# Attention weights of the first key block in a ring of six units instead of four, and a second table of rotations turned only when it can be taken up

## The chip, the cores and the metric

The kernel runs on one core of a Trainium2 chip. The metric is the device time of one execution in microseconds (us), lower is better. Its engines, as the profile names them: PE (TensorE, matrix products; PEld is its weight load), DVE (VectorE), ACT (ScalarE), POOL (GpSimd), SP (SyncE, which here only starts transfers, DMAs). SBUF is the working memory, PSUM the eight banks of 512 fp32 columns into which PE writes.

## The reference

Four batch elements of 512 rows by 512 features (`x`) go through eight blocks, each `x = layernorm(x + block(x))`: a small state-space network (width 64, four layers), a four-bit linear map, then attention 1, a gated FFN, attention 2, a routed mixture of low-rank experts, attention 3 and a wide gated FFN (1792). The three attentions have 32 query heads, 8 key/value heads and a head width of 16; all three are causal. Cut to the attention:

```python
q = rope(x @ Wq); k = rope(x @ Wk); v = x @ Wv        # 32, 8, 8 heads of 16
scores = einsum("bkgqd,bkmd->bkgqm", q, k) / sqrt(16)  # attention 1: / 16
scores = where(causal, scores, -inf)
out = einsum("bkgqm,bkmd->bkgqd", softmax(scores), v) @ Wo
```

## The kernel before, in words

**Stages.** The batch elements run one after the other through each attention, so there are 12 pairs (attention, element), numbered n = 0 to 11 (`NIT`). Each n has 8 groups, one for each key/value head with its four query heads; group g = 8n + head, 96 in all. First come the state-space layers and the four-bit map of the four elements (called quarters q in the layers), last the wide FFN. The dense products, FFNs and projections of the neighbouring n are dealt out between the groups of n as side work (`side_work`).

**One group.** The scores are computed twice. The first time (`max_scores`, units `max`, 10 for each group, 20 for each pair p of groups) DVE takes their maxima (L2144); for a unit with the diagonal ACT first writes a mask into the bank (`mask_first`, "preset", L1720). The maxima of a pair are split (`split_max`), turned by PE (`turn_shift`), copied (`take_shift`) and sent through DRAM back into extra rows of the queries. The second time (`exp_scores`, units `exp`, 10 a group, L1420) PE computes scores less their maximum, and ACT takes the exponential into `probs` (`weights_of`, L1731). Units 0 to 3 hold key block 0 (one head each, 512 queries), units 4 to 7 the key blocks 1 and 3, units 8 and 9 key block 2. POOL clears what is above the diagonal (`cut`, L1959), and PE multiplies by the values (`weigh`, L1435) in two halves: half 0 takes key block 0 (`pv` 0), half 1 the others (`pv` 1). ACT copies the result out (`out_heads`, L1739).

**The room for the weights.** `probs` holds ten units of 512 columns, unit i in place i. So unit i < 4 of group g may be written only when half 0 of group g - 1 is through PE, and unit i > 3 when half 1 is:

```python
if g:
    act.wait_ge(made["pv_full"], counted("pv_full", g - 1, int(i > 3)))
```

**The layers.** For each layer l and quarter q: statistics (DVE `hs`, L2114 to L2120), POOL `hr`, scaling (ACT `hx`, L1631), a turn (PE `th`, L1309, out to SBUF by ACT), the scan (DVE `mod`, L2127 to L2129), then PE `hm` (L1337), again statistics and a turn, and the widening (PE `f`, L1343, two a layer) and narrowing products (PE `hd`, L1348 and L1352). The final turn gives `last` (L1360), the output product. The four accumulators of the layers hold four of the eight banks, so the turns and `f` have the other four.

**The rotation tables.** The tables of cosines and sines arrive as rows (`ropet`), are turned by PE into a bank (`turn_tables`, units `tabs`, L1309) and copied by ACT into `cs` (`rotations`, L1754 to L1757). Table 1 serves attention 1, table 2 attention 2 and 3. ACT may copy table 2 only after the last rotation of n = 3, since `cs` is in use until then.

**Order of the work.** Nothing is scheduled at run time: every engine has a fixed list, and a wait holds all that stands behind it in the list. The lists are made when the program is built, by `Flow.try_out`: it deals the steps of the plan out with assumed durations (`pieces`), takes on each engine the step that could begin first, and honours the dependences in `order_of` and the room in the eight banks (`room`): a step that needs a bank takes one whose last content has been taken up (`released`). `tabs` and the layers' steps may go ahead of the plan (`AHEAD`). For a bank that is given by the planner the program waits on the step that releases it (`bank_for`).

Of the kernel before, what the change touches and what calls it, by code (L numbers as in the profile page):

```python
# [9 lines left out]
ACT = mybir.ActivationFunctionType  # L10
# [60 lines left out]
def exp_unit(i):  # L71

    if i < 4:
        return [(0, i, 0)]
    if i < 8:
        return [(1, i - 4, 0), (3, i - 4, 3 * P)]
    return [(2, 2 * (i - 8), 0), (2, 2 * (i - 8) + 1, 2 * P)]
# [271 lines left out]
def order_of(engine, name, k):  # L349
# [84 lines left out]
    if name == "probs":  # L434
        return [("exp_full", k), ("pv_full", (n - 1, int(k[1] > 3))) if n else ("y_full", ("l", 0, TJ - 1))]
# [45 lines left out]
    if name == "tabs":  # L481
        return [("load_rope", k)]
# [433 lines left out]
def program(nc, ins, out, kinds):  # L916
    assert list(kinds) == ALL
    flow = FLOW
    with ExitStack() as ctx:
        def sb(name, shape, dt):  # L920
            return ctx.enter_context(nc.sbuf_tensor(name, shape, dt))
# [48 lines left out]
        ropet = sb("ropet", [P, TJ, 2, 64], F32)  # L970
# [6 lines left out]
        a = sb("a", [P, D], F32)  # L977
        t1 = sb("t1", [P, S], F32)
        t2 = sb("t2", [P, S], F32)
        r = sb("r", [P, CH, S], F32)  # L980
# [10 lines left out]
        big1 = sb("big1", [P, 14336], F32)  # L991
# [3 lines left out]
        probs = big1[:, 7680:12800]  # L995
        qp = big1[:, 12800:14336].bitcast(BF16).rearrange("p (k s t) -> p k s t", k=2, s=3)
# [12 lines left out]
        wgu = big1[:].rearrange("p (g c k n) -> p g c k n", g=M3 // 2, c=DC, k=2)  # L1009
# [69 lines left out]
        def probs_of(key):  # L1079

            lo, hi, at = ((0, 2048, 0), (2048, 4096, 0), (4096, 5120, 0), (2048, 4096, 3 * P))[key]
            return probs[:, lo:hi].rearrange("p (h t) -> p h t", h=GQ)[:, :, at:at + S - key * P]
# [4 lines left out]
        def _(sp):  # L1087
# [19 lines left out]
            def load_rope(A):  # L1107
                if A > 1:
                    sp.wait_ge(made["tabs_full"], counted("tabs_full", 1))
                sp.dma_start(ropet[:], ins[f"attn{A}_rope"]).then_inc(rope_in, 16)  # L1110
# [187 lines left out]
        def _(pe):  # L1298
# [113 lines left out]
            def exp_scores(g, i):  # L1412
                p = g // 2
                if i == 0 and g % 2 == 0:
                    pe.wait_ge(shift_in[p % 3], 16 * (p // 3 + 1))
                    if g == 0:
                        pe.wait_ge(ready, 1)
                bank = bank_for("exp", g, i)
                for key, h, at in exp_unit(i):
                    mm = pe.matmul(bank[:, at:at + S - key * P], kt[0:SROWS, p % 3, g % 2, key * P:(key + 1) * P],  # L1420
                                   qt[0:SROWS, g % 6, h, key * P:S], start=(at == 0), stop=True, skip_group_check=True)
                mm.then_inc(made["exp_full"], 1)

            def weigh(g, half_):
# [8 lines left out]
                for key in (1, 3, 2) if half_ else (0,):  # L1433
                    for h in range(GQ):
                        mm = pe.matmul(bank_of("pv", g)[32 * h:32 * h + 32, key * P:S], vs[:, n % 2, key, g % 8, :],  # L1435
                                       probs_of(key)[:, h], start=(key == 0), stop=(key == 2), skip_group_check=True)
# [179 lines left out]
        def _(act):  # L1616
# [107 lines left out]
            def weights_of(g, i):  # L1724
                n = g // 8
                if g:
                    act.wait_ge(made["pv_full"], counted("pv_full", g - 1, int(i > 3)))
                elif i == 0:
                    act.wait_ge(made["y_full"], counted("y_full", "l", 0, TJ - 1))
                act.wait_ge(made["exp_full"], counted("exp_full", g, i))  # L1730
                act.activation(probs[:, i * S:(i + 1) * S], bank_of("exp", g, i), ACT.Exp,  # L1731
# [83 lines left out]
            def squares(n):  # L1815
                act.wait_ge(made["xn"], counted("xn", "d", n))
                act.wait_ge(made["lo"], counted("lo", NIT - 1, CHUNKS[-1]))
                for j in range(TJ):
# [3 lines left out]
                    act.activation(a[:, 0:D], x_rows(n, j), ACT.Square, accum_out=ssq[:, k:k + 1]).then_inc(made["sq"], 1)  # L1822
# [80 lines left out]
        def _(pool):  # L1903
# [51 lines left out]
            def cut(g, key):  # L1955

                pool.wait_ge(made["probs"], counted("probs", g, KEY_ENDS[key]))
                block_ = probs_of(key)[:, :, 0:P]
# [614 lines left out]
```

## Time and profile before

| | before |
| --- | --- |
| median of 3 runs | 2340.5 us (2339.69 to 2342.32) |
| the profiled execution: its own time | 2339.58 us |
| its span in the trace | 2337.9 us |
| PE busy (products) | 2211.4 us, 95% of the span |
| DVE, ACT, POOL busy | 1423.1, 1237.7, 509.3 us |
| mean granted clock of TensorE | 0.972 |

The span is the time from the first to the last instruction; the 1.7 us between it and the execution's own time are outside the program. A busy PE in these views has modelled ends: products are pipelined, and each is shown somewhat longer than it keeps the next from starting. The granted clock is given as a share of full speed (2.4 GHz); its lower level is half of it.

### The profile page before, as it was taken

The page shows a single profiled execution, that of the slowest core. Times are in us where ns is not written, and L with a number is a line of the kernel's source. Part 1 is how long each engine was busy: PE and PEld are TensorE (multiplying, and loading weights), DVE is VectorE, ACT ScalarE, POOL GpSimd, SP SyncE. Part 2 cuts the span into 40 slices and gives each one's busy share as a digit, 9 for nine tenths or more (in the row PEclk, how much of TensorE's full clock was granted, in tenths as well). Part 3 has the DMA queues.
Part 4 walks back from the last instruction along what each step waited for, and adds up shares of the span by engine and source line. Part 5 has one row for each costly group of instructions (what it writes and reads, how often), then busy time and mean ns, then how long its engine had stood idle before and what let it go on. Part 6 is the DMA issues. An engine that isn't in the chain of part 4 may idle for free.

```text
span 2337.9 us, 35726 instructions
## 1 busy us (share of the span) xinstructions
PE 2211.4 (95%) x12528; PEld 1175.9 (50%) x12528; DVE 1423.1 (61%) x3153; ACT 1237.7 (53%) x2313; POOL 509.3 (22%) x646
## 2 busy tenths in 40 slices
PE   6788798999999999999999999999998999999998
PEld 5565454545455454555555555554543444444443
DVE  7756778867768586687878887878832222221222
ACT  6466597756657475676767675787761101011010
POOL 4422233223313132232323231322220000000000
PEclk8779899999999999999999999999999999999999
DMA  5001233412313132332423243333222000000000
GB/s 183 1 1 38 82 100 109 154 51 82 111 40 121 36 118 66 97 105 70 128 68 110 67 127 106 119 97 102 74 83 71 5 14 0 18 0 5 14 0 18
DMA packets 135777, 163.24 MB, mean 70 GB/s; under 512 B 42272, under 2 KB 97696, under 8 KB 135328
## 3 DMA queue, kind: packets, MB, share of 16 engines
q1 hardware_dynamic: 135600, 160.97, 22.3%
q8 instruction: 101, 1.65, 0.3%
q14 instruction: 76, 0.62, 0.1%
HBM read 94.19 MB, written 53.35 MB: 63 GB/s over the span
## 4 chain that ended last, share of the span: by engine, by line
PE 81%; DVE 6%; ACT 4%; DMA 4%; issue 2%; SPq 1%; POOL 1%; POOLq 0%; ACTq 0%; DVEq 0%
PE ps L1537 16%; PE ps L1435 9%; PE ps L1465 8%; PE ps L1548 8%; PE ps L1420 7%; PE ps L1444 7%; PE ps L1490 5%; PE ps L1390 3%; PE ps L1395 3%; PE ps L1499 2%; PE ps L1522 2%; PE ps L1309 2%; PE ps L1475 2%; PE ps L1401 2%; ACT big L1731 1%
## 5 line engine op out<-in xcount | busy, mean ns | idle before, releaser
L2144 DVE TENSOR_REDUCE peaks<-ps 128x4 f32<-128x512 f32 x960 | 623.3, 681 | 213.7 <-PE ps L1390 114.6
L1731 ACT ACTIVATE big<-ps 128x512 f32<-128x512 f32 x960 | 548.2, 603 | 295.0 <-PE ps L1420 219.9
L1959 POOL TENSOR_SCALAR_AFFINE_SELECT big<-big 128x512 f32<-128x512 f32 x384 | 257.0, 682 | 869.3 <-ACT big L1731 868.0
L1537 PE MATMUL ps<-xt,big 128*128 128x512 f32 x896 | 390.1, 593 | 2.9 <-issue 2.9
L1420 PE MATMUL ps<-big 99*128 99x512 bf16 (+3 forms) x1536 | 337.9, 300 | 12.4 <-DMA big<-scr_shift 4.6
L1537 PEld LDWEIGHTS ps<-xt,big 128*128 128x128 f32 x896 | 168.8, 190 | 209.2 <-issue 208.0
L1840 ACT ACTIVATE t<-ps 128x512 f32<-128x512 f32 x56 | 33.5, 598 | 453.4 <-PE ps L1537 453.4
L1465 PE MATMUL ps<-xt,big 128*128 128x512 f32 x480 | 246.1, 607 | 1.4 <-ACT xt L1746 1.1
L1435 PE MATMUL ps<-big,vs 128*32 128x512 f32 (+3 forms) x3072 | 239.5, 439 | 6.7 <-POOL big L1959 5.6
L1720 ACT ACTIVATE ps<-cbf 128x512 f32<-128x512 bf16 x384 | 230.4, 605 | 19.2 <-DVE peaks L2144 15.4
L2200 DVE SCALAR_TENSOR_TENSOR t<-rest,t 128x512 f32<-128x512 f32 x56 | 38.7, 691 | 280.1 <-PE ps L1537 275.7
L1420 PEld LDWEIGHTS ps<-big 99*128 99x128 bf16 x1536 | 133.0, 97 | 131.3 <-issue 67.5
L1390 PEld LDWEIGHTS ps<-big 96*128 96x128 bf16 x1536 | 112.4, 98 | 156.5 <-issue 115.6
L1548 PE MATMUL ps<-wf,big 128*128 128x512 f32 x384 | 167.8, 593 | 1.6 <-DVE big L2201 1.6
L1390 PE MATMUL ps<-big 96*128 96x128 bf16 x1536 | 150.8, 220 | 4.5 <-ACT ps L1720 4.0
L1395 PE MATMUL ps<-big 96*128 96x256 bf16 x768 | 148.5, 275 | 4.2 <-DVE peaks L2144 2.3
L1435 PEld LDWEIGHTS ps<-big,vs 128*32 128x32 f32 x3072 | 80.8, 109 | 105.4 <-issue 81.9
L1490 PE MATMUL ps<-xt,wf 128*128 128x512 f32 x256 | 125.4, 607 | 0.0
L1947 POOL TENSOR_TENSOR sm<-sm,half 128x1 f32<-128x1 f32 x16 | 8.7, 543 | 527.1 <-DVE sm L2220 527.1
L1395 PEld LDWEIGHTS ps<-big 96*128 96x128 bf16 x768 | 68.2, 99 | 102.1 <-issue 90.1
L1548 PEld LDWEIGHTS ps<-wf,big 128*128 128x128 f32 x384 | 72.6, 190 | 92.5 <-issue 89.9
L1444 PE MATMUL ps<-big 128*128 128x512 f32 x192 | 98.3, 611 | 5.9 <-DVE big L2172 5.9
(232 smaller groups left out, 2917.8 us busy)
## 6 DMA issues: line engine op xcount, KB each, us to landing
big<-scr_q SPq DMA_DIRECT2D x96, 384.0 KB, 4.0
scr_q<-big SPq DMA_DIRECT2D x48, 384.0 KB, 2.9
scr_q<-big SPq DMA_DIRECT2D x48, 256.0 KB, 3.0
recb<-scr_sums SPq DMA_DIRECT2D x96, 128.0 KB
big<-scr_k SPq DMA_DIRECT2D x48, 192.0 KB, 3.3
big<-in_ffn_gu SPq DMA_DIRECT2D x14, 512.0 KB, 5.1
scr_q<-big SPq DMA_DIRECT2D x48, 128.0 KB, 2.9
ctxt<-ots SPq DMA_DIRECT2D x192, 32.0 KB, 2.0
```

The costliest lines, as they stand in the source:

```text
L1390: mm = pe.matmul(bank_of("max", p, u)[:, h * P:(h + 1) * P], of(h, at), against(at, at + 1), start=False, stop=True, skip_group_check=True)
L1395: mm = pe.matmul(bank[:, 2 * P * k:2 * P * (k + 1)], of(at, 2 + k), against(0, 2), start=(k == 0), stop=True, skip_group_check=True)
L1420: mm = pe.matmul(bank[:, at:at + S - key * P], kt[0:SROWS, p % 3, g % 2, key * P:(key + 1) * P], qt[0:SROWS, g % 6, h, key * P:S], start=( ...
L1435: mm = pe.matmul(bank_of("pv", g)[32 * h:32 * h + 32, key * P:S], vs[:, n % 2, key, g % 8, :], probs_of(key)[:, h], start=(key == 0), stop ...
L1444: mm = pe.matmul(bank_of("dense", n, j), heads[n % 2][:, c, j * P:(j + 1) * P], wd[:, c, :], start=(c == 0), stop=(c == DC - 1))
L1465: mm = pe.matmul(bank_of("proj", n, c), wp[:, k, c * P:(c + 1) * P], xt[:, k, :], start=(k == 0), stop=(k == DC - 1))
L1490: mm = pe.matmul(bank_of(kind, n, m), wf1[:, c, at + m * P:at + (m + 1) * P], xt[:, c, :], start=(c == 0), stop=(c == DC - 1))
L1537: mm = pe.matmul(bank_of(kind, n, m), wgu[:, m // 2, c, way, m % 2 * P:(m % 2 + 1) * P], xt[:, c, :], start=(c == 0), stop=(c == DC - 1))
L1548: mm = pe.matmul(bank_of("down3", n, j), ht3[:, m, j * P:(j + 1) * P], wdn[:, m, :] if m < 12 else wdn2[:, m - 12, :], start=(m == 0), sto ...
L1731: act.activation(probs[:, i * S:(i + 1) * S], bank_of("exp", g, i), ACT.Exp, scale=1.0 / 16 if attn_of(n) == 1 else 0.25).then_inc(made["p ...
L1959: pool.affine_select(block_, block_, [[0, GQ], [1, P]], ALU.is_ge, zero, base=0, channel_multiplier=-1).then_inc(made["cut"], 1)
L2144: dve.tensor_reduce(to, blocks, AX.X, ALU.max, negate=True).then_inc(made["negmax"], 1)
```

## The change

Five things are changed; the computation is the same.

1. `probs` has twelve units of room instead of ten. Key block 0 has six places: an even group writes its units 0 to 3 to places 0, 1, 2, 3, an odd group to places 4, 5, 2, 3 (`place`), with the heads dealt so that the four places that hold a group's block stand side by side (`exp_unit`, `probs_of`). Units 4 to 9 have places 6 to 11.
2. The exponential of units 0 and 1 therefore waits for half 0 of group g - 2; units 2 and 3 still for half 0 of group g - 1, units 4 to 9 for its half 1.
3. The turn of the second rotation table has a new dependence in the planner: it comes after the last rotation of n = 3, as ACT's copy of it does.
4. To make room for the two units (4 KB in each partition), `ropet` lies in `t2` and the scratch of the squares `a` is replaced by a half of `cs`.
5. The lists of all engines are made anew with the new dependences.

```diff
+def place(g, i):
+    return i + 2 if i > 3 else i if g % 2 == 0 else (4, 5, 2, 3)[i]
+
-def exp_unit(i):
+def exp_unit(g, i):
     if i < 4:
-        return [(0, i, 0)]
+        return [(0, place(g, i) - 2 * (g % 2), 0)]
...
     if name == "probs":
-        return [("exp_full", k), ("pv_full", (n - 1, int(k[1] > 3))) if n else ("y_full", ("l", 0, TJ - 1))]
+        return [("exp_full", k), ("pv_full", (n - 1 - int(k[1] < 2), int(k[1] > 3))) if n > int(k[1] < 2) else ("y_full", ("l", 0, TJ - 1))]
...
     if name == "tabs":
-        return [("load_rope", k)]
+        return [("load_rope", k)] + ([("rope", (NB - 1, CHUNKS[-1]))] if n == 2 else [])
...
-        ropet = sb("ropet", [P, TJ, 2, 64], F32)
-        a = sb("a", [P, D], F32)
+        ropet = t2[:].rearrange("p (j w k) -> p j w k", j=TJ, w=2)
...
-        big1 = sb("big1", [P, 14336], F32)
+        big1 = sb("big1", [P, 15360], F32)
...
-        def probs_of(key):
-            lo, hi, at = ((0, 2048, 0), (2048, 4096, 0), (4096, 5120, 0), (2048, 4096, 3 * P))[key]
+        def probs_of(g, key):
+            first = 1024 * (g % 2)
+            lo, hi, at = ((first, first + 2048, 0), (3072, 5120, 0), (5120, 6144, 0), (3072, 5120, 3 * P))[key]
...
             def weights_of(g, i):
                 n = g // 8
-                if g:
-                    act.wait_ge(made["pv_full"], counted("pv_full", g - 1, int(i > 3)))
-                elif i == 0:
+                back = g - 1 - int(i < 2)
+                if back >= 0:
+                    act.wait_ge(made["pv_full"], counted("pv_full", back, int(i > 3)))
+                else:
                     act.wait_ge(made["y_full"], counted("y_full", "l", 0, TJ - 1))
                 act.wait_ge(made["exp_full"], counted("exp_full", g, i))
-                act.activation(probs[:, i * S:(i + 1) * S], bank_of("exp", g, i), ACT.Exp,
+                act.activation(probs[:, place(g, i) * S:(place(g, i) + 1) * S], bank_of("exp", g, i), ACT.Exp,
...
-                    act.activation(a[:, 0:D], x_rows(n, j), ACT.Square, accum_out=ssq[:, k:k + 1]).then_inc(made["sq"], 1)
+                    act.activation(cs[:, 0, :], x_rows(n, j), ACT.Square, accum_out=ssq[:, k:k + 1]).then_inc(made["sq"], 1)
```

No instruction is added or removed on any engine; what changes is the order. The new file is seven lines longer in the engines' part, so L1309 of before is L1315 of the change, L1343 is L1349, L1352 is L1358, L1360 is L1366, L1390 is L1396, L1395 is L1401, L1720 is L1726, L1731 is L1738 and L1739 is L1746.

**The turn of table 2, on PE.** Before, among the layers (the turn of the table reads `ropet`; the turn with `wf` is a layer's, `th`):

```order
L1348 MATMUL ps<-wf,ident 128x256 [waits f_ft]
L1352 MATMUL ps<-wf,big1 128x64 x8
L1309 MATMUL ps<-ident,ropet 128x128 [waits f_ut,rope_in]
L1309 MATMUL ps<-ident,ropet 128x128 x3
L1309 MATMUL ps<-ident,wf 128x128 [waits f_rotations,f_hx]
L1309 MATMUL ps<-ident,wf 128x128 x3
```

With the change, between dense products of n = 1 and maxima of n = 2, in group 19 of 96:

```order
L1450 MATMUL ps<-big2 128x512
L1426 MATMUL ps<-big1 128x512 [waits f_cosine]
L1450 MATMUL ps<-big2 128x512 [waits f_probs,dense_in,f_ctn]
L1315 MATMUL ps<-ident,t2 128x128 [waits f_probs,rope_in]
L1315 MATMUL ps<-ident,t2 128x128 x3
L1396 MATMUL ps<-big1 128x128 [waits f_preset]
L1396 MATMUL ps<-big1 128x128 x3
```

The turn moved from the 31st step of PE's list to the 813th. ACT's copy of table 2 keeps its place in ACT's list.

**The first pair's maxima, on PE.** `big1` alone is a unit of maxima, `ident,wf` or `ident,big2` a layer's turn that waits for ACT's scaling (`f_hx`), `ident,x` the turn of element 1 for its projections, which waits for its normalization (`f_nx`), `wf,big2` 128x512 an output product `last`, `big2` L1337 a mixing step. Before:

```order
L1337 MATMUL ps<-sm,big2 128x64 [waits f_sel,f_mod]
L1337 MATMUL ps<-sm,big2 128x64 x3
L1390 MATMUL ps<-big1 128x128 [waits f_preset]
L1390 MATMUL ps<-big1 128x128 x3
L1309 MATMUL ps<-ident,wf 128x128 [waits f_y16,f_hx]
L1309 MATMUL ps<-ident,wf 128x128 x3
L1395 MATMUL ps<-big1 128x256 [waits f_hx]
L1395 MATMUL ps<-big1 128x256
L1390 MATMUL ps<-big1 128x128 [waits f_preset]
L1390 MATMUL ps<-big1 128x128 x3
L1395 MATMUL ps<-big1 128x256 [waits f_negmax]
```

With the change:

```order
L1396 MATMUL ps<-big1 128x128 [waits f_preset]
L1396 MATMUL ps<-big1 128x128 x3
L1366 MATMUL ps<-wf,big2 128x512 [waits f_ft,w_out,f_ut]
L1366 MATMUL ps<-wf,big2 128x512 [waits f_negmax,w_out,f_ut]
L1401 MATMUL ps<-big1 128x256 [waits f_negmax]
L1401 MATMUL ps<-big1 128x256
L1396 MATMUL ps<-big1 128x128 [waits f_preset]
L1396 MATMUL ps<-big1 128x128 x3
L1401 MATMUL ps<-big1 128x256 [waits f_negmax]
L1401 MATMUL ps<-big1 128x256
L1366 MATMUL ps<-wf,big2 128x512 [waits f_negmax,w_out,f_ut]
L1315 MATMUL ps<-ident,x 128x128 [waits f_negmax,f_nx]
```

A layer's turn (quarter 2's final one) stood behind unit 3 of the maxima; it now stands before the four-bit products of element 1, and output products of element 2 have its place. The next turn of the layers (quarter 3) comes after unit 6 and one turn of element 1. All along the layers the steps of quarters 1 to 3 stand further ahead: before the first output product (L1360) there are six more of them (two turns, three widening products, one narrowing product), before the first unit of maxima six (two turns, two widening products, a mixing step and a narrowing product, the scan on DVE for it too), and before the first `exp` unit a narrowing product, a turn and two units of maxima. From group 48 to group 79 PE's list is the same as before.

**Around the end of a group, on ACT.** L1731 is an exponential, L1739 the copy of a group's result, L1720 a mask. Before, at group 50:

```order
L1720 ACTIVATE ps<-cbf 128x512 [waits f_negmax]
L1720 ACTIVATE ps<-cbf 128x512 [waits f_cosine]
L1787 ACTIVATE big1<-r 128x512 [waits parts_out1,f_rope]
L1731 ACTIVATE big1<-ps 128x512 [waits f_exp_full,f_pv_full]
L1720 ACTIVATE ps<-cbf 128x512 [waits f_probs]
L1791 ACTIVATE big1<-rest 128x512 [waits f_rest]
L1739 ACTIVATE ots<-ps 128x512 [waits heads_in,sums_in,f_pv_full]
```

With the change:

```order
L1726 ACTIVATE ps<-cbf 128x512 [waits f_negmax]
L1738 ACTIVATE big1<-ps 128x512 [waits f_exp_full,f_pv_full]
L1726 ACTIVATE ps<-cbf 128x512 [waits f_cosine]
L1794 ACTIVATE big1<-r 128x512 [waits parts_out1,f_rope]
L1726 ACTIVATE ps<-cbf 128x512 [waits f_probs]
L1798 ACTIVATE big1<-rest 128x512 [waits f_rest]
L1746 ACTIVATE ots<-ps 128x512 [waits heads_in,sums_in,f_pv_full]
```

The next group's first exponential moved ahead of a mask and of the first part of a rotated chunk.

## Rows read from the trace of the kernel before

**Rows 1.** The page: PE's busy time, and the granted clock in 40 slices.

```profile
PE 2211.4 (95%) x12528; PEld 1175.9 (50%) x12528; DVE 1423.1 (61%) x3153; ACT 1237.7 (53%) x2313; POOL 509.3 (22%) x646
...
PEclk8779899999999999999999999999999999999999
```

**Rows 2.** Windows: stretch and length; busy us of each engine; granted clock; DMA share, GB/s.

```profile
40.00:200.00 160.00, 121.99 (x562) 87.00 (x562) 106.64 (x347) 93.11 (x192) 65.99 (x73) 0.77 0.01 2
200.00:300.00 100.00, 76.64 (x387) 48.55 (x385) 70.74 (x185) 59.34 (x106) 28.74 (x34) 0.86 0.23 70
300.00:480.00 180.00, 168.32 (x1312) 89.38 (x1316) 150.50 (x298) 147.08 (x271) 56.73 (x76) 1.00 0.39 124
480.00:1440.00 960.00, 949.01 (x6452) 513.13 (x6440) 717.98 (x1441) 619.07 (x1140) 257.37 (x318) 1.00 0.28 86
1440.00:1750.00 310.00, 293.76 (x2264) 154.80 (x2262) 226.39 (x443) 229.70 (x437) 82.73 (x116) 0.99 0.33 100
```

**Rows 3.** PE timeline in the middle: start us, duration us, instruction, count.

```profile
718.88 1.02 PE L1465 MATMUL ps<-xt,big 128*128 128x512 f32 x2
...
719.75 0.38 PE L1395 MATMUL ps<-big 96*128 96x256 bf16 x2
...
719.97 0.38 PE L1420 MATMUL ps<-big 99*128 99x512 bf16 x1
```

**Rows 4.** The waits of ACT from 480 to 1440 us: total us, times, longest.

```profile
ACT big L1731 <- PE ps L1435: 56.1, 35, 3.7
```

**Rows 5.** The tile `ropet`: duration ns min/median/max, first and last start us.

```profile
L1309 PE MATMUL ps<-ident,ropet x8: 421/421/421, 51.2 to 68.1; 128*128 128x128 f32 x8
```

**Rows 6.** The tile `cs`, ACT's copies of both tables, same columns.

```profile
L1754 ACT ACTIVATE cs<-ps x2: 577/578/580, 56.2 to 593.0; 64x512 f32<-64x512 f32 x2
```

**Rows 7.** The waits of PE from 40 to 200 us.

```profile
PE ps L1309 <- ACT wf L1631: 12.5, 7, 4.8
```

**Rows 8.** PE timeline in the layers.

```profile
72.36 3.78 PE L1343 MATMUL ps<-big,wf 128*128 128x512 f32 x4 [0.87 <-ACT big L1692]
...
135.94 0.63 PE L1309 MATMUL ps<-ident,big 128*128 128x128 f32 x4 [2.28 <-ACT big L1697]
...
141.20 3.51 PE L1352 MATMUL ps<-wf,big 128*128 128x64 f32 x16
...
172.05 4.22 PE L1360 MATMUL ps<-wf,big 128*128 128x512 f32 x8
...
178.70 1.94 PE L1343 MATMUL ps<-big,wf 128*128 128x512 f32 x4
...
194.18 1.89 PE L1352 MATMUL ps<-wf,big 128*128 128x64 f32 x16
```

**Rows 9.** PE timeline, first pair's maxima and the first `exp` unit.

```profile
248.26 0.39 PE L1390 MATMUL ps<-big 96*128 96x128 bf16 x4
254.69 1.12 PE L1309 MATMUL ps<-ident,wf 128*128 128x128 f32 x4 [6.05 <-ACT wf L1631]
...
292.93 0.38 PE L1420 MATMUL ps<-big 99*128 99x512 bf16 x1
```

**Rows 10.** DVE timeline in the same stretch.

```profile
242.89 1.48 DVE L2127 TENSOR_TENSOR big<-big,wf 128x512 f32<-128x512 f32 x1
244.40 1.28 DVE L2128 TENSOR_TENSOR_SCAN big<-phz,big 128x512 f32<-128x512 f32 x1
245.72 0.69 DVE L2129 TENSOR_TENSOR big<-big,wf 128x512 f32<-128x512 f32 x1
...
263.44 0.69 DVE L2246 TENSOR_TENSOR x<-ps,x 128x512 f32<-128x512 f32 x1 [5.27 <-PE ps L1360]
...
271.91 0.62 DVE L2114 BATCH_NORM_STATS2 hstat<-ps 128x6 f32<-128x64 f32 x4 [1.95 <-PE ps L1352]
```

**Rows 11.** The waits of PE from 1440 to 1750 us.

```profile
PE ps L1420 <- DMA big<-scr_shift: 4.2, 2, 2.8
...
PE ps L1435 <- POOL big L1959: 2.9, 8, 0.6
```

More of the change, by code:

```diff
@@ L994, in program @@
         kt = big1[:, 6144:7680].bitcast(BF16).rearrange("p (k h t) -> p k h t", k=3, h=2)
-        probs = big1[:, 7680:12800]
-        qp = big1[:, 12800:14336].bitcast(BF16).rearrange("p (k s t) -> p k s t", k=2, s=3)
+        probs = big1[:, 7680:13824]
+        qp = big1[:, 13824:15360].bitcast(BF16).rearrange("p (k s t) -> p k s t", k=2, s=3)
         peaks = sb("peaks", [P, 2, 2, GQ, TJ, 4], F32)
@@ L1008, in program @@
         halves, tanhs = (t1[:, 0:512], t2[:, 0:512]), (rest[:, 0, :], rest[:, 1, :])
-        wgu = big1[:].rearrange("p (g c k n) -> p g c k n", g=M3 // 2, c=DC, k=2)
+        wgu = big1[:, 0:14336].rearrange("p (g c k n) -> p g c k n", g=M3 // 2, c=DC, k=2)
         wdn = wf[:].rearrange("p (m n) -> p m n", m=12)
@@ L1109, in load_rope @@
                     sp.wait_ge(made["tabs_full"], counted("tabs_full", 1))
-                sp.dma_start(ropet[:], ins[f"attn{A}_rope"]).then_inc(rope_in, 16)
+                sp.dma_start(ropet, ins[f"attn{A}_rope"]).then_inc(rope_in, 16)
             def load_ffn1():
@@ L1418, in exp_scores @@
                 bank = bank_for("exp", g, i)
-                for key, h, at in exp_unit(i):
+                for key, h, at in exp_unit(g, i):
                     mm = pe.matmul(bank[:, at:at + S - key * P], kt[0:SROWS, p % 3, g % 2, key * P:(key + 1) * P],
@@ L1435, in weigh @@
                         mm = pe.matmul(bank_of("pv", g)[32 * h:32 * h + 32, key * P:S], vs[:, n % 2, key, g % 8, :],
-                                       probs_of(key)[:, h], start=(key == 0), stop=(key == 2), skip_group_check=True)
+                                       probs_of(g, key)[:, h], start=(key == 0), stop=(key == 2), skip_group_check=True)
                 mm.then_inc(made["pv_full"], 1)
@@ L1957, in cut @@
                 pool.wait_ge(made["probs"], counted("probs", g, KEY_ENDS[key]))
-                block_ = probs_of(key)[:, :, 0:P]
+                block_ = probs_of(g, key)[:, :, 0:P]
                 pool.affine_select(block_, block_, [[0, GQ], [1, P]], ALU.is_ge, zero, base=0, channel_multiplier=-1
```

## Prediction

> **What bounds the kernel now.** I read the page first. PE's products fill 95% of the span and its granted clock is 90% or more from the sixth of 40 slices on [rows 1]. The windows then say where PE is short of work [rows 2]: from 480 to 1440 us it is busy 949.0 of 960 us; from 40 to 200 us 122.0 of 160, at a mean granted clock of 0.77; from 200 to 300 us 76.6 of 100; from 300 to 480 us 168.3 of 180; from 1440 to 1750 us 293.8 of 310. A change of order alone can only win PE's gaps: 38.0 + 23.4 + 11.7 + 11.0 + 16.2 us in these five stretches, and what the lower clock costs early.
>
> Busy has modelled ends, so I checked the middle by start times [rows 3]. The two fp32 instructions begun at 718.88 are followed at 719.75, 0.87 us later, and the two of 256 columns begun there are followed after 0.22 us. That is 1024 fp32 columns in 0.87 us, then 512 bf16 columns in 0.22: at these rates each stream starts when the one before it has gone through, so the middle is really full. In the same 960 us ACT waits 56.1 us for the products with the values before an exponential [rows 4], and PE has 11.0 us of gaps in all. So nearly all of this wait is hidden behind PE's own work.
>
> One resource is held for long. Table 2 is turned at 68.1 us at the latest [rows 5], and ACT begins to copy it at 593.0 [rows 6]. One bank of eight is idle for some 525 us, in the layers one of the four that the accumulators leave.
>
> **The change, part by part.**
>
> *(a) The ring of six.* The first two exponentials of a group no longer wait for the last group's half 0. From 480 to 1440 us this frees ACT, not PE: PE does the same columns there, partly in the very same order. I count 0. Its ends are 0 and -11.0 (all PE gaps of the stretch); if PE's work did not cover ACT, up to the 56.1 us of wait would be on the path. Should ACT run ahead, the next thing late is PE's `exp` product itself.
>
> *(b) The bank in the layers.* PE's largest wait from 40 to 200 us is for scaled rows from ACT, 12.5 us in 7 waits [rows 7]; only the wait of 2.28 us at 135.94 [rows 8], ended by the activation of a widening product whose result does not feed that turn, looks like a wait for a bank. So the layers are bound by chains from engine to engine, and a fourth bank helps only in that more steps of other quarters can lie in the holes. That has a price: six more steps stand ahead of the first output product of element 0, on which everything later depends. Two turns of 0.6 us (as the turn at 135.94), three widening products at 0.9 (four instructions, two products, take 1.8 us by their starts in the full-clock case; the row's 1.94 us bounds them), and one narrowing product (its 16 instructions 1.89 us, and about 0.4 for the bias) make 6.2 us at full clock. At half clock the rows are 3.78 and 3.51 us in place of 1.94 and 1.89 [rows 8], so the six make about 11.4. Against them stand 38.0 us of gaps [rows 2], most of them shorter than 3 us, and some 1 us for the table's turn that is gone. The ends are 0 (all in holes) and +11.4 (all on the chain). I take half of the full-clock price, +3.0, since the gaps are five times the work, but short and ended by waits of this same chain.
>
> *(c) The first pair's maxima.* Before, PE stands 6.05 us until 254.69 at a turn of quarter 2, with maxima behind it [rows 9]; ACT's scaled rows for it are late because DVE did a scan first and then the sums of element 1. With the change that turn is already done, output products stand there, and the scan (1.48 + 1.28 + 0.69 = 3.45 us [rows 10]) is gone from before the sums. What is late next is the normalization of element 1, which hangs on these sums, so the gain here is the scan, -3.4 us, and not 6.05. Behind it DVE must now do quarter 3's scan (1.28 and twice 0.69, 2.7 us), one more statistic, a sum and a rotation step, some 6 us more before the first pair is split; it had 5.27 + 1.95 us idle there [rows 10], so I cost them at nothing. If that cover is gone, all 6 us come back. Ends: -6.0 and +2.6.
>
> *(d) Work done before the first `exp` unit (292.93 [rows 9]).* From there PE is nearly full, so what is done earlier is won: a narrowing product 2.3, a turn 0.6, two units of maxima 0.2 each by start times [rows 3]: -3.1 us, if (b) and (c) hold. Ends: 0 and -3.1.
>
> *(e) 300 to 480 us.* PE has 11.7 us of gaps. There are eight banks in place of seven and ACT is freer. I take -1.5, since DVE is busy 150.5 of the 180 us [rows 2] and gets no help. Ends: +2 and -11.7.
>
> *(f) 1440 to 1750 us.* Of 16.2 us of gaps, 4.2 are the transfer of the shifts and 2.9 POOL's clearing before the value products [rows 11]. The ring touches neither, only when ACT gets to the exponentials that POOL waits for. I take -0.5; ends: +2 and -8.
>
> *(g) The moved turn, squares and tables in borrowed rooms.* One turn of four instructions at 0.42 us, overlapped, in PE's full stretch: +0.5, and some -1 early, already in (b). The squares and `ropet` wait for nothing that is late. No transfer moves by more than a few places. 0.
>
> Sum: 3.0 - 3.4 - 3.1 - 1.5 - 0.5 = -5.5 us. The profiled execution took 2339.58 us, 1.7 of it outside the span, so it gives 2334.1; the median of the runs shown is 0.9 higher, and I forecast **2335.0 us** for the median.
>
> The clock needs a word. From 40 to 200 us it was granted at 0.77, a mix of the levels 1.2 and 2.4 GHz; the same 16 narrowing instructions took 3.51 us after gaps and 1.89 us in fuller company [rows 8]. The Trainium skill (TensorE: Matmul & The Clock Gate, What's actually happening) says that the throttled state is the default and that activity releases it. By that rule fuller holes would raise the clock and the sum would be larger than mine, which keeps it as it was.
>
> **The rivals.**
>
> *No change.* The first exponentials are tied to the layers' chain of element 0 and to DVE's 20 maxima of the first pair, and what is won in (c) and (d) is paid in (b) at half clock. For it: DVE idles only 7.2 us in that chain, and the middle is full whatever happens. Time: -3.4 - 3.1 + 6.2 - 1 = -1.3, so 2339.
>
> *Slower.* The place is the layers before the first output product. The list puts other quarters' steps before element 0's, and PE holds its list: if the six steps fall at half clock and their inputs arrive late, the chain moves by 11.4 us, and (c) cannot return more than 3.4, with (d) 0 because DVE's extra 6 us are no longer covered. Time: +11.4 - 3.4 = +8, so about 2348.5. It decides if element 0's output comes more than about 7 us later than before. For it: most gaps are ended by exactly this chain. Against: they sum to 38 us.
>
> *Larger gain: the clock rises.* With a granted clock of 0.86 from 40 to 200 us (that of the next stretch [rows 2]) the 122.0 us of products would take 109.2, 12.8 less. Some two thirds of it on the chain, with my -5.5, give -14: 2326.5.
>
> *Larger gain: the middle had slack.* The 513.1 us of weight loads are only 53% of the 960 us [rows 2]. If PE had slack there, the 56.1 us of ACT's waits would be worth something; a quarter of them gives -14, and with the other terms -19.5: 2321. The Trainium skill (Perfetto Trace Analysis, Identifying the Most-Contended Engine) calls busy time of products a bad measure for TensorE and wants the share of weight loads looked at. By that rule there is room; the starts in [rows 3] say that there is none.
>
> **How the numbers follow.** This kernel's measurement tells about 0.2%, 4.7 us, from no change. Chances: forecast (gain of about 5 to 10) 0.42, no change 0.34, slower 0.15, clock 0.07, slack in the middle 0.02. Faster by over 0.2% is 0.42 + 0.07 + 0.02 = 0.51, though the forecast lies only 0.8 us past that line, and so I move 0.03 to within: 0.48, 0.37, 0.15. The range must reach into the clock case and, on the other side, through no change well into the slower case: 2326 to 2346, with 1 in 10 outside on either side.
>
> **What would show it.** Right: the table is turned near 590 us; no wait of 6 us in PE between 245 and 260 us; the first exponential 2 to 6 us earlier than 293; PE busy from 480 to 1440 us still within 2 us of 949, at the same span of groups; ACT's waits for value products (L1435) well under 56.1 us with no gain from it. The first output product of element 0 (172.05 us before [rows 8]) within 4 us. Wrong: that product over 7 us later, or a mean clock in 40 to 200 us off 0.77 by over 0.05 either way, or the time from the first exponential of group 8 to the end changed by more than 5 us, which would say that the middle or the end, and not the start, decides.

## The result, and the profile after

| | before | with the change |
| --- | --- | --- |
| median of 7 runs, in turns on one chip | 2341.65 us (2339.69 to 2344.53) | 2330.57 us (2322.07 to 2334.29) |
| ratio, 95% interval | | 0.9946 [0.9932, 0.9960] |
| the profiled execution, its span | 2339.58, 2337.9 us | 2330.87, 2329.2 us |
| mean granted clock of TensorE | 0.972 | 0.974 |

The change is faster by 0.54% (medians: 11.1 us; the forecast was 5.5). The two profiled executions differ by 8.7 us: that of before lies 2.1 us under its median, that of the change 0.3 above. The page of the change, the lines that answer to [rows 1]:

```profile
PE 2211.0 (95%) x12523; PEld 1174.1 (50%) x12528; DVE 1427.9 (61%) x3153; ACT 1236.2 (53%) x2313; POOL 512.7 (22%) x646
...
PEclk8789899999999999999999999999999999999999
```

Its windows, as in [rows 2]:

```profile
40.00:200.00 160.00, 119.22 (x588) 86.29 (x587) 112.08 (x369) 99.75 (x206) 71.43 (x77) 0.78 0.01 3
200.00:300.00 100.00, 85.28 (x483) 51.63 (x485) 77.47 (x188) 68.06 (x123) 30.63 (x35) 0.93 0.24 75
300.00:480.00 180.00, 165.44 (x1241) 87.99 (x1243) 146.97 (x281) 140.99 (x256) 58.79 (x74) 0.99 0.39 123
480.00:1440.00 960.00, 949.09 (x6486) 513.51 (x6484) 724.50 (x1453) 618.79 (x1144) 254.25 (x317) 1.00 0.29 88
1440.00:1750.00 310.00, 295.15 (x2190) 153.37 (x2190) 217.66 (x423) 223.14 (x426) 80.39 (x112) 0.97 0.34 102
```

PE's work is the same, 2211.0 us of products against 2211.4. One window stands out: 200 to 300 us, busy 85.3 us in place of 76.6 and clock 0.93 in place of 0.86. The middle is as full as it was, 949.1 against 949.0. The first `exp` unit is where the gain can be read as a time. ACT loads its exponential table just before the first exponential; of the program's three table loads only this one stands at the exponential's line, so the row can be read like the hand of a clock (columns: duration minimum, median, maximum, first and last start). First before, then the change:

```profile
L1731 ACT ACT_TABLE_LOAD  x1: 1283/1283/1283, 293.4 to 293.4; - x1
```

```profile
L1738 ACT ACT_TABLE_LOAD  x1: 1283/1283/1283, 284.5 to 284.5; - x1
```

It starts 8.9 us earlier, and the whole span is 8.7 us shorter. Following the first exponential of later groups through both timelines of ACT (ten exponentials make a group, so group 8 begins with the 81st), group 8 comes 5.6 us earlier (397.0 and 391.4), group 16 11.1 (543.9 and 532.7), group 80 9.0 (1549.6 and 1540.6). From the table load to the end both take the same time, 2044.5 and 2044.7 us. So the gain is made before the attention begins. In the PE timeline of the change, where [rows 9] had the wait of 6.05 us:

```profile
242.74 3.78 PE L1349 MATMUL ps<-big,wf 128*128 128x512 f32 x4 [3.23 <-ACT big L1698]
...
251.41 1.94 PE L1366 MATMUL ps<-wf,big 128*128 128x512 f32 x4
...
254.64 1.10 PE L1366 MATMUL ps<-wf,big 128*128 128x512 f32 x2 [0.30 <-DVE peaks L2151]
255.57 0.60 PE L1315 MATMUL ps<-ident,x 128*128 128x128 f32 x4
```

Output products fill the place of the wait, and the first turn of element 1 for its projections stands at 255.57. PE's largest waits from 200 to 300 us, before and then with the change:

```profile
PE ps L1309 <- ACT x L1640: 6.6, 2, 5.7
PE ps L1309 <- ACT wf L1631: 6.0, 1, 6.0
```

```profile
PE ps L1349 <- ACT big L1698: 4.2, 2, 3.2
PE ps L1396 <- ACT ps L1726: 3.3, 4, 1.1
```

The two new operations of order are in the trace as written. The table's turns (`t` is `ropet`'s new place) and ACT's copies, as in [rows 5, 6], now lie a third of a microsecond apart at 582 us:

```profile
L1315 PE MATMUL ps<-ident,t x8: 272/347/421, 53.3 to 581.6; 128*128 128x128 f32 x8
```

```profile
L1761 ACT ACTIVATE cs<-ps x2: 576/583/590, 58.3 to 581.9; 64x512 f32<-64x512 f32 x2
```

And the first output product, which the six more steps of the layers could have pushed back, stands at the same time (172.05 before [rows 8]):

```profile
L1366 PE MATMUL ps<-wf,big x32: 590/592/1061, 172.0 to 365.4; 128*128 128x512 f32 x32
```

That it stands still is a coincidence. The first scan of the layers is the 17th step of DVE's list in both kernels, ahead of any difference of the lists, and the change reached it 2.2 us later. The delay comes from PE's 32 products that start at 12 us: 4.86 us before, 7.06 in the change, and 3.76 in e3 below, whose lists are word for word before's. First before, then the change, the products and the scan:

```profile
12.22 4.86 PE L1323 MATMUL ps<-wf,xt 128*128 128x64 f32 x32 [0.78 <-ACT xt L1621]
39.07 1.28 DVE L2128 TENSOR_TENSOR_SCAN big<-phz,big 128x512 f32<-128x512 f32 x1
```

```profile
12.27 7.06 PE L1329 MATMUL ps<-wf,xt 128*128 128x64 f32 x32 [0.78 <-ACT xt L1627]
41.26 1.28 DVE L2135 TENSOR_TENSOR_SCAN big<-phz,big 128x512 f32<-128x512 f32 x1
```

The granted clock from 12 to 20 us reads 0.67 in before and 1.00 in the other two, so the rows do not settle the cause of the late start. Counted from the first scan, the first output product comes after 132.9 us before and after 130.7 with the change, 2.2 us sooner.

The ring's side is in ACT's waits from 480 to 1440 us. Of before two rows that [rows 4] leaves out (exponentials that wait for scores, and the copy of a group's result), then the change:

```profile
ACT big L1731 <- PE ps L1420: 170.2, 224, 3.6
ACT ots L1739 <- PE ps L1435: 45.8, 49, 3.9
```

```profile
ACT big L1738 <- PE ps L1426: 187.6, 255, 2.5
ACT ots L1746 <- PE ps L1441: 90.9, 47, 4.8
```

The 56.1 us that exponentials waited for value products are gone, and the copies of results, next in ACT's list, wait 90.9 in place of 45.8 for the very same products. Exponentials wait 17.4 us longer for their own scores (L1420, now L1426). The wait changed its owner: 56.1 + 45.8 + 170.2 = 272.1 us before, 90.9 + 187.6 = 278.5 after.

### The profile page after: what moved, and what is told of

It is laid out like the page before. It is cut to its first block, busy times and chain, and to the rows that moved or that the text cites. A ratio compares the mean times of both kernels' runs of the same rounds, so it can differ in the third digit from the quotient of the medians.

```text
span 2329.2 us, 35733 instructions
## 1 busy us (share of the span) xinstructions
PE 2211.0 (95%) x12523; PEld 1174.1 (50%) x12528; DVE 1427.9 (61%) x3153; ACT 1236.2 (53%) x2313; POOL 512.7 (22%) x646
## 4 chain that ended last, share of the span: by engine, by line
PE 81%; DVE 7%; ACT 4%; DMA 3%; issue 3%; SPq 1%; POOL 1%; POOLq 0%; ACTq 0%; DVEq 0%
PE ps L1543 16%; PE ps L1441 8%; PE ps L1471 8%; PE ps L1554 8%; PE ps L1426 7%; PE ps L1450 7%; PE ps L1496 5%; PE ps L1396 3%; PE ps L1401 3%; PE ps L1505 2%; PE ps L1528 2%; PE ps L1315 2%; PE ps L1481 2%; DVE peaks L2151 2%; PE ps L1407 2%
## 5 line engine op out<-in xcount | busy, mean ns | idle before, releaser
L1738 ACT ACTIVATE big<-ps 128x512 f32<-128x512 f32 x960 | 546.8, 602 | 247.7 <-PE ps L1426 242.1
L1426 PE MATMUL ps<-big 99*128 99x512 bf16 (+3 forms) x1536 | 339.9, 302 | 11.8 <-DMA big<-scr_shift 5.8
L1726 ACT ACTIVATE ps<-cbf 128x512 f32<-128x512 bf16 x384 | 232.5, 606 | 24.6 <-DVE peaks L2151 22.6
L1426 PEld LDWEIGHTS ps<-big 99*128 99x128 bf16 x1536 | 134.5, 98 | 119.8 <-issue 55.6
L1396 PEld LDWEIGHTS ps<-big 96*128 96x128 bf16 x1536 | 111.9, 98 | 163.0 <-issue 122.5
L1396 PE MATMUL ps<-big 96*128 96x128 bf16 x1536 | 151.3, 221 | 7.4 <-ACT ps L1726 6.9
L1401 PE MATMUL ps<-big 96*128 96x256 bf16 x768 | 149.1, 275 | 0.8 <-DVE peaks L2151 0.7
L1746 ACT ACTIVATE ots<-ps 128x512 f32<-128x512 f32 x96 | 57.5, 599 | 127.2 <-PE ps L1441 126.3
L1401 PEld LDWEIGHTS ps<-big 96*128 96x128 bf16 x768 | 69.0, 99 | 105.5 <-issue 95.4
```

Source lines behind the costliest of these rows:

```text
L1396: mm = pe.matmul(bank_of("max", p, u)[:, h * P:(h + 1) * P], of(h, at), against(at, at + 1), start=False, stop=True, skip_group_check=True)
L1401: mm = pe.matmul(bank[:, 2 * P * k:2 * P * (k + 1)], of(at, 2 + k), against(0, 2), start=(k == 0), stop=True, skip_group_check=True)
L1726: act.activation(bank_of("max", p, u).rearrange("p (h k) -> p h k", h=GQ), mask_q.unsqueeze(1).broadcast_to((P, GQ, P)), ACT.Copy).then_in ...
L1738: act.activation(probs[:, place(g, i) * S:(place(g, i) + 1) * S], bank_of("exp", g, i), ACT.Exp, scale=1.0 / 16 if attn_of(n) == 1 else 0. ...
```

## The experiments

Two theories. **The bank:** the table's turn held one of four free banks among the layers; with the fourth, PE's list there has other quarters' work in its holes. **The ring:** exponentials no longer wait for value products. A third stands beside them, and e7 to e12 are made for it: **the lists' chance**, that any new assumption of the planner deals steps anew, and what that does is luck. Every ratio is to before, run in turns with it on the same chip; e1 to e4, e5 to e8 and e9 to e12 are three sessions on three chips, each with its own 17 to 35 runs of before, and each experiment has 5 to 12 runs.

**e1: the moved turn alone.** Before, with the new dependence only.

```diff
     if name == "tabs":
-        return [("load_rope", k)]
+        return [("load_rope", k)] + ([("rope", (NB - 1, CHUNKS[-1]))] if n == 2 else [])
```

> The kernel before with only the new dependence of the second table's turn (four places for key block 0, the waits of before, lists made anew). Theory A (the bank that the table held among the layers makes the gain): 9 to 12 us under the kernel before, first exponential at 283 to 286 us as in the change. Rival B (the ring makes it): within 2 us of the kernel before. Rival C (any new list differs by this much): anything between -12 and +6.

Measured: 0.9967 [0.9950, 0.9984], 7.7 us, first exponential at 283.6. The turn alone is a gain of 0.33%; the time lies between what theory A and rival B expect, the first exponential where theory A has it.

**e2: the ring alone.** The change with that one line as it was.

```diff
     if name == "tabs":
-        return [("load_rope", k)] + ([("rope", (NB - 1, CHUNKS[-1]))] if n == 2 else [])
+        return [("load_rope", k)]
```

> The change without the new dependence of the table's turn: six places, freed waits, the turn early as before. Theory A: within 2 us of the kernel before, first exponential at 290 to 295 us. Rival B: 8 us or more under it. Rival C: anything.

Measured: 0.9988 [0.9972, 1.0004], first exponential at 290.0. Not told from nothing.

**e3: the ring's places and freed waits, with before's lists.** As e2, and the planner keeps the old dependence, so that every list is word for word before's and only the waits differ.

```diff
     if name == "probs":
-        return [("exp_full", k), ("pv_full", (n - 1 - int(k[1] < 2), int(k[1] > 3))) if n > int(k[1] < 2) else ("y_full", ("l", 0, TJ - 1))]
+        return [("exp_full", k), ("pv_full", (n - 1, int(k[1] > 3))) if n else ("y_full", ("l", 0, TJ - 1))]
```

> The lists of the kernel before on every engine, but six places and the freed waits of the exponentials. Theory A: 0 to -1 us against the kernel before, and the waits of the exponentials for the value products (56.1 us from 480 to 1440 us before) fall by over half without any effect. Rival B, if it is the wait itself that costs: -5 us or more.

Measured: 0.9997 [0.9980, 1.0014]. The middle's window and ACT's waits in it:

```profile
480.00:1440.00 960.00, 950.58 (x6476) 514.14 (x6475) 721.95 (x1452) 617.27 (x1142) 255.76 (x318) 1.00 0.29 87
```

```profile
ACT big L1738 <- PE ps L1426: 179.3, 237, 3.6
ACT ots L1746 <- PE ps L1441: 93.5, 50, 4.8
```

No exponential waits for value products any more. Without any change of order the copy has taken over 47.7 us of the wait and the scores 9.1, together 56.8 of the 56.1 that were freed, and the time is not told from before's. The wait of 56.1 us was slack that PE's full queue covered.

**e4: the change's lists with the old waits.**

```diff
-                back = g - 1 - int(i < 2)
+                back = g - 1
```

> The lists of the change on every engine, but units 0 and 1 wait for half 0 of the last group as before. Theory A: as fast as the change, 9 to 12 us under the kernel before, since nothing waits for ACT in the middle; at most 2 us slower, because in these lists the next group's first exponential stands ahead of masks and would now hold them. Rival B, if the freed wait matters with the new lists: 5 us or more slower than the change.

Measured: 1.0016 [1.0001, 1.0031], 0.7% or some 16 us above the change: theory A's "at most 2 us slower" is refuted, rival B came. ACT and PE from 480 to 1440 us:

```profile
ACT big L1738 <- PE ps L1441: 102.8, 48, 4.2
```

```profile
PE ps L1396 <- ACT ps L1726: 10.1, 11, 1.2
```

In these lists an exponential stands ahead of a mask (the order rows at group 50 show it). If it waits, the mask behind it waits too, and PE, which is full, stands for the mask: PE is busy 939.5 us in the window in place of 949.1. The change's profile has no such wait of PE for masks in this window. So the freed wait is worth nothing that these runs can tell where the list was made without it, and is needed where the list counts on it. This is a test of a list that the old kernel would never run, not a measure of the ring's gain.

**e5: the change without the bank.** The turn comes late, as in the change, but the planner may not give bank 3 to any step on PE from the 31st on until the last narrowing product of the layers.

```diff
         for b in BANKS:
             when = 0
+            if b == 3 and 30 <= len(self.order["PE"]) and ("hd_full", (NL - 1, NB - 1)) not in ended:
+                continue
```

> The change, but the planner may not use bank 3 from PE's 31st step until the last narrowing product of the layers; after that all eight banks. This leaves the layers three banks, as before, and gives the attention eight. Theory A (the bank counts among the layers): the gain of the table's part is lost, 0 to 4 us under the kernel before, first exponential at 288 to 294 us. Rival (the eighth bank counts in the attention up to 593 us): 8 us or more under it. Rival C (any new list): anything.

**e6: the bank held later.** The change, with the turn allowed as soon as the layers are through.

```diff
     if name == "tabs":
-        return [("load_rope", k)] + ([("rope", (NB - 1, CHUNKS[-1]))] if n == 2 else [])
+        return [("load_rope", k)] + ([("hd_full", (NL - 1, NB - 1))] if n == 2 else [])
```

> The change, but the second table is turned right after the layers (PE's 213th step) and holds its bank until 590 us: eight banks among the layers, seven in the attention up to there. Theory A: as the change, 8 to 12 us under the kernel before, first exponential at 282 to 287 us. Rival (the attention's bank): within 3 us of the kernel before.

Measured: e5 0.9986 [0.9969, 1.0002], e6 0.9938 [0.9915, 0.9961]. The window 200 to 300 us of e5, of e6, and e6's turns of the tables:

```profile
200.00:300.00 100.00, 76.88 (x385) 49.94 (x385) 70.17 (x177) 57.92 (x104) 27.11 (x31) 0.85 0.22 70
```

```profile
200.00:300.00 100.00, 83.44 (x501) 50.32 (x502) 79.49 (x193) 69.66 (x125) 32.45 (x38) 0.98 0.25 78
```

```profile
L1315 PE MATMUL ps<-ident,t x8: 272/350/421, 53.3 to 277.7; 128*128 128x128 f32 x8
```

Taking the bank from the layers takes the gain away, although everything else of the change is there: from the first scan to the table load e5 takes 254.8 us, before 254.3, the change 243.2. (Its first exponential, 297.4, is later than the 288 to 294 expected.) Holding the bank from 277.7 us on, through the first two and a half elements of the attention, costs nothing that shows in the total. In one stretch a difference does show: from group 8 to group 16 the seven kernels that hold the bank there take 142.2 to 146.9 us, the seven that have it free 138.2 to 141.6 (e5 the least). Most of this is given back elsewhere: from the table load to the end the five that hold it take 2044.5 to 2047.4 us and the six that do not 2041.5 to 2045.9 (without e4, e7 and e10, which lose in other ways). So the gain of the table's part is made among the layers; whether the eighth bank is worth a microsecond or two in the attention stays open.

**e7 to e12: the lists' chance.** `TURN`, the 450 ns that the planner assumes for a turn on PE, is set 10 ns lower or higher. No instruction, wait or place of the program is touched, only what the planner believes. e7: before with 440; e8: the change with 460; e9: e1 with 460; e10: e2 with 440; e11: e6 with 460; e12: the change once more, unaltered.

```diff
-TURN, ROWS_ACT, ROWS_DVE = 450, 640, 730
+TURN, ROWS_ACT, ROWS_DVE = 460, 640, 730
```

> The kernel before with one assumed duration of the planner changed, a turn of 440 ns in place of 450, which reorders some of every list and changes nothing else. It measures what a list made anew does by chance. Theory A: within 3 us of the kernel before. Rival C (chance of the lists explains the gain): 5 us or more from it, either way.

> The change with a turn of 460 ns assumed in place of 450; the same control on the other side. Theory A: still 8 to 13 us under the kernel before. Rival C: the gain is halved or gone.

> The kernel before with the new dependence of the table's turn alone and 460 ns assumed for a turn; the partner of the change with 460 ns, which has the ring too. Theory A, as the runs so far leave it (bank among the layers about -0.35%, ring about -0.15% by its lists): 8 to 12 us under the kernel before, and the partner 3 to 6 us faster. Rival (the ring is worth nothing, list chance made its share): within 2 us of the partner, at -14 to -17 us.

> The ring without the new dependence, 440 ns assumed; the partner of the kernel before with 440 ns, which took 6 us more than the kernel before. If the ring helps through its lists: 3 us or more under that partner, at +3 us or less against the kernel before. If the ring is worth nothing: +5 to +7 us.

> The change with the table turned right after the layers and 460 ns assumed: both edits that came out fastest so far. Theory A (only the layers' banks count, the rest is chance of the lists): 11 to 19 us under the kernel before. If the eighth bank counts in the attention after all: less than 8 us.

> The change once more, beside these three. It took 0.54% less than the kernel before, interval 0.40 to 0.68%; the same is expected, 9 to 16 us less.

All fourteen profiles, with three times in us (the first scan of the layers, the first output product, ACT's table load before the first exponential) and the two stretches between them.

| kernel | banks free among the layers | ratio to before | first scan | first output product | table load | scan to product | product to load |
| --- | --- | --- | --- | --- | --- | --- | --- |
| before | 3 | 1 | 39.1 | 172.0 | 293.4 | 132.9 | 121.4 |
| e2 ring alone | 3 | 0.9988 [0.9972, 1.0004] | 36.7 | 168.2 | 288.7 | 131.5 | 120.5 |
| e3 ring, old lists | 3 | 0.9997 [0.9980, 1.0014] | 36.0 | 169.0 | 289.1 | 133.0 | 120.1 |
| e5 bank blocked | 3 | 0.9986 [0.9969, 1.0002] | 41.3 | 174.3 | 296.1 | 133.0 | 121.8 |
| e7 before, 440 | 3 | 1.0030 [1.0015, 1.0044] | 39.0 | 168.9 | 293.4 | 129.9 | 124.5 |
| e10 ring alone, 440 | 3 | 1.0004 [0.9989, 1.0020] | 39.1 | 172.1 | 293.5 | 133.0 | 121.4 |
| change | 4 | 0.9946 [0.9932, 0.9960] | 41.3 | 172.0 | 284.5 | 130.7 | 112.5 |
| e12 change again | 4 | 0.9939 [0.9921, 0.9957] | 41.2 | 171.9 | 286.1 | 130.7 | 114.2 |
| e1 turn alone | 4 | 0.9967 [0.9950, 0.9984] | 41.2 | 172.0 | 282.3 | 130.8 | 110.3 |
| e4 new lists, old waits | 4 | 1.0016 [1.0001, 1.0031] | 41.1 | 171.5 | 285.8 | 130.4 | 114.3 |
| e6 turn after the layers | 4 | 0.9938 [0.9915, 0.9961] | 41.2 | 172.1 | 282.4 | 130.9 | 110.3 |
| e8 change, 460 | 4 | 0.9928 [0.9912, 0.9943] | 36.8 | 164.3 | 278.1 | 127.5 | 113.8 |
| e9 turn alone, 460 | 4 | 0.9924 [0.9908, 0.9939] | 39.0 | 165.5 | 278.1 | 126.5 | 112.6 |
| e11 turn after layers, 460 | 4 | 0.9917 [0.9900, 0.9934] | 37.2 | 165.1 | 279.5 | 127.9 | 114.4 |

The last column is the cleanest reading of the study: 120.1 to 124.5 us in every kernel with three banks, 110.3 to 114.4 in every kernel with four. Counted from the first scan, which takes out the chance of the start, it is 252.0 to 254.8 us to the table load against 239.1 to 244.9. Apart from e4, which loses in the middle what it won here, the two families are apart in the ratio as well: 0.9986 and above with three banks, 0.9967 and below with four.

The families hold fewer lists than kernels. Up to ACT's first exponential all engines have the same lists in the six kernels with three banks (in e5 but for the turn of the table); the same again in the change, e12, e1, e4 and e6 (in e6 but for that turn); and once more in e8, e9 and e11 (in e11 up to PE's 200th step). So the column shows one list with three banks in six executions, and two lists with four banks, in five and in three. That tells the lists from the chance of an execution, and the gain of four banks from the luck of one list. A second list with three banks was not run there: 440 alters before's lists only behind this stretch, from PE's 324th step on (the first `exp` unit is the 218th). Against luck on that side stands e5, where the planner comes back to before's very list although the turn is late. The planner gives before the same lists up to the first exponential with 430, 460 and 470 ns too; these kernels were not run.

Within a family 10 ns of assumption move the time by 0.2 to 0.4% (before to e7 +0.30, e2 to e10 +0.16, change to e8 -0.2, e1 to e9 -0.43, e6 to e11 -0.2). What e7 loses it loses in the attention: from the table load to the end it takes 2057.3 us, before 2044.5. This chance is near the size of the effect itself, so the ratio of one relisted kernel proves nothing; the stretch and e5 carry the argument.

The ring's own share can be read in four pairs that differ by it: before to e2 -0.12%, e7 to e10 -0.26, e1 to the change -0.21, e9 to e8 +0.04. Each lies within the chance of the lists, and three of them compare runs of different sessions. Their mean, -0.14%, is an indication and not a measurement. The two runs made for this question answered it in opposite ways by their own expectations: e9 came within 1 us of its partner, as it should if the ring is worth nothing, and e10 6 us under its partner, as it should if the ring helps. The ring's share of the gain stays open.

Against what was expected: e2, at 2.8 us under before, and e8, e9 and e6, at 16.9, 17.8 and 14.5, gained more than theory A had them gain, and e11, at 19.5, just left its range; e7, at 7.0 us over before where theory A had it within 3, went to rival C. e3, e5 and e12 took the times expected. So theory A was right on the place of the gain and too narrow on what chance does.

e11 is the fastest of all, 2323.45 us at the median, 0.83% below before and some 0.25% below the change. It asks only that the turn wait for the end of the layers. Its first output product comes 7 us earlier, but 4.1 us of that are the earlier first scan; 2.8 us are the list's (127.9 against 130.7). In e8 and e9 the list's part is 3.2 and 4.2 us. Why 460 does that stays open; the runs show it for all three kernels with that number.

## Why the prediction was right, and where it was too small

The direction was right, and the time is inside the range; the likeliest case was named, and undersized by half (5.5 us, measured 11.1 by the medians).

*(a) The ring, 0.* Confirmed, by e3 above all, as far as its waits go. The mark "waits for L1435 well under 56.1 us with no gain" came out, and PE's 949.1 us are within 2 of 949.0. I named PE's `exp` product as what would be late next; that is 17.4 us of it (9.1 in e3), and the larger part, which I had not written, is the copy of the result, 45.8 to 90.9 us.

*(b) The six steps among the layers, +3.0.* This is the term that was mis-sized, with the wrong sign: from the first scan to the first output product the change takes 130.7 us and before 132.9, -2.2. The five executions of the change's list have 130.4 to 130.9, the six of before's 129.9 to 133.0, so the term lies between 0 and about -2, and not at +3. That the product stands at 172.0 us in both is the late start of 2.2 us. I had asked whether the six steps fall in holes or on the chain of element 0, and not whether that chain can gain by the bank too. Which of its steps gains was not followed.

*(c), (d) The first pair and the work done before, -6.5.* The terms of (d) add up to 3.3 and not 3.1, so this should have been -6.7, and the sum -5.7. Between the first output product and the first exponential the profiles show 121.4 us before and 112.5 with the change, -8.9. Mechanism and place are as said: no wait of 6 us, products in its stead. The size is 2.2 larger. The clock from 200 to 300 us was 0.93 in place of 0.86, and I had costed the clock at nothing after 200 us. The Trainium skill (TensorE: Matmul & The Clock Gate, What's actually happening) says that activity releases the clock. Between the two families of kernels the trace agrees: 0.85 to 0.88 at 76.5 to 79.4 us busy with three banks, 0.90 to 0.98 at 81.9 to 85.3 with four; among the four-bank kernels it does not: 0.98 at 83.4 and 83.6 us and 0.91 and 0.93 at 85.2 and 85.3. I had drawn its case for the layers alone, where the clock hardly rose (0.78 against 0.77). Whether the 2.2 us are the clock's or those of the fuller list no run separates.

With (b) at -2.2 and this at -8.9, the stretch from the first scan to the first exponential gives -11.1 where my steps gave -3.5. That is the error. The span of the profiled execution is shorter by only 8.7, since it began 2.2 us late and took 0.2 more after the table load, where (e) and (f) gave -2.0. The forecast is inside the range with (b) too high by 5.2 us and (e) and (f) not shown, which hid 2.0 of it.

*(e) 300 to 480 us, -1.5.* Not shown. From the first exponential to that of group 8 the change took 105.6 us against 102.3, and from there to group 16 141.4 against 146.9, together -2.2. The same kernel run again (e12) has -0.5 for the two.

*(f) The end, -0.5, and (g), 0.* From group 80 to the end 788.5 us against 788.2, nothing to tell from 0. From group 8 to the end 1937.8 against 1940.9, inside my 5 us; in e12 1934.9, outside them. That mark was badly placed: what lies ahead of group 8 differs by 3.9 us between two executions of one program (105.6 and 109.5).

*The rivals.* The slower case needed the first output product 7 us late; it did not come late at all. "No change" was wrong in the same term: it priced (b) at 6.2 us. "The middle had slack" is refuted by e3: the freed waits gave PE nothing, though the weight loads take only 514.1 of 960 us. "The clock rises" has its rise in another window than it named, and what that is worth in time is not known.

## What to carry to other kernels

A bank that is filled early and read late shows no cost where it is filled; look for the stretch in which the others have to do without it, and let the early step wait until that stretch is over. A wait on an engine beside the full one is not worth removing by itself: the next instructions inherit it, here all of 56.1 us. Where a planner deals the order anew, measure the edit with the old order too, and jog the planner by a hair in both kernels, before a few tenths of a per cent are put down to the edit. Then see whether the jog reached the stretch in question: here 440 left before's layers as they were.

## What had not been expected of the hardware

**The clock falls inside the attention, too.** e7 and e10, both with 440 ns, reach group 16 at 552.4 and 549.5 us; before reaches it at 543.9, and no other kernel later than 545.8. From 350 to 360 us of e7, of e10, and of before:

```profile
350.00:360.00 10.00, 9.10 (x64) 4.33 (x65) 5.06 (x8) 6.13 (x12) 2.78 (x5) 0.53 0.66 212
```

```profile
350.00:360.00 10.00, 8.80 (x63) 4.24 (x63) 5.06 (x8) 6.33 (x13) 3.09 (x5) 0.53 0.65 212
```

```profile
350.00:360.00 10.00, 8.09 (x77) 3.61 (x76) 6.55 (x12) 9.40 (x19) 4.18 (x6) 1.00 0.59 188
```

The granted clock is near its lower level for most of ten microseconds, in two kernels at the same place. It is the longest fall but not the only one: read in slices of 10 us from 300 to 400 us, every kernel with four banks but the change itself has at least one slice between 0.83 and 0.90, and before, e2 and e3 have none. Ahead of the fall PE waited for ACT in e7's timeline:

```profile
349.05 0.60 PE L1420 MATMUL ps<-big 99*128 99x384 bf16 x2 [1.13 <-ACT big L1731]
350.51 0.61 PE L1390 MATMUL ps<-big 96*128 96x128 bf16 x4 [0.86 <-ACT ps L1720]
```

From 340 to 350 us PE is busy 8.0 us there and 9.3 in before, where the clock stayed full. But the change is busy only 7.8 us in that slice and keeps the full clock in it and in the next, so busy time in a slice does not tell which list falls. Over 300 to 400 us the mean is 0.92 in both, 1.00 in before. The later group 16 may be the small waits, the clock or both; how large each part is was not separated.

**The same kernel's early stretch varies by more than its total seems to allow.** The change and e12 are one program. Their windows from 300 to 400 us:

```profile
300.00:400.00 100.00, 88.83 (x710) 45.83 (x711) 83.20 (x161) 83.96 (x154) 33.04 (x44) 1.00 0.40 123
```

```profile
300.00:400.00 100.00, 89.80 (x703) 46.91 (x705) 79.63 (x159) 82.45 (x153) 29.18 (x40) 0.95 0.35 105
```

Group 8 begins at 391.4 us in one and at 397.0 in the other, and the spans differ by 2.7 us. Before and e3, whose lists are the same, differ by 4.3 us at the first exponential, and 3.0 of these are there at the first scan (39.1 and 36.0). So a term of 2 or 3 us can't be read from one profile of each kernel. (b), (e) and (f) are of that size; only their sign or their smallness can be told, and that from several profiles.
